# Expert stage: the Silu outputs turned by a transposing DMA from ACT's queue instead of by PE

## The reference, cut to what matters

```
gate_scores = sigmoid(x @ gate_w.T + balance_bias)
topk_scores, topk_idx = top_k(gate_scores, 2)          # 8 experts, 2 for each token
h = silu(einsum('td,ehd->teh', xf, w1))                # 512 -> 1024
expert_out = einsum('teh,edh->ted', h, w2)             # 1024 -> 512
out = x + sum over the two chosen experts of gate * expert_out
```

## Time and profile before

| | us |
|---|---|
| median of three runs | 609.57 |
| lowest and highest | 607.44 and 611.71 |
| the profiled execution | 608.84 |
| its span | 607.0 |
| PE busy, whole span | 516.3 (85%) |
| DVE, ACT, POOL busy | 402.2, 286.3, 116.2 |

### The profile page before, as it was taken

How to read it: one execution, slowest core, us unless ns; L and a number is a source line. 1 busy time by engine, 2 the same in 40 slices (tenths; PEclk the granted TensorE clock), 3 DMA queues, 4 the chain that set the end, 5 groups by cost and what they waited for, 6 DMA issues and landing times.

```text
span 607.0 us, 11363 instructions
## 1 busy us (share of the span) xinstructions
PE 516.3 (85%) x3769; PEld 305.8 (50%) x3770; DVE 402.2 (66%) x897; ACT 286.3 (47%) x449; POOL 116.2 (19%) x89
## 2 busy tenths in 40 slices
PE   5789999999989898954640699999999999999993
PEld 2664657465565675734430344545555445545441
DVE  3789778937979787875976567666563737683330
ACT  0652868685276484747410354453444525552120
POOL 1212113103150301101272002111211121121112
PEclk9899999999999899986855789999999999999997
DMA  8991505000009991062167247876482674623212
GB/s 324 391 382 52 209 8 202 2 1 2 1 23 383 381 381 36 30 208 105 53 246 272 81 152 229 228 220 191 103 238 74 187 192 118 230 52 52 35 35 35
DMA packets 32785, 93.23 MB, mean 154 GB/s; under 512 B 2896, under 2 KB 4080, under 8 KB 28656
## 3 DMA queue, kind: packets, MB, share of 16 engines
q1 hardware_dynamic: 23984, 74.81, 34.3%
q0 software_dynamic: 4304, 9.77, 8.5%
q10 hardware_dynamic: 4464, 8.22, 4.5%
HBM read 63.36 MB, written 29.43 MB: 153 GB/s over the span
## 4 chain that ended last, share of the span: by engine, by line
PE 68%; issue 10%; DVE 8%; ACT 7%; POOL 3%; DMA 2%; SPq 0%; ACTq 0%; POOLq 0%; DVEq 0%
PE bank L685 19%; PE bank L703 18%; PE bank L342 9%; PE bank L510 4%; PE bank L494 2%; PE bank L424 2%; PE bank L544 2%; PE bank L360 2%; PE bank L454 2%; PE bank L404 2%; PE bank L603 2%; PE bank L534 2%; PE bank L475 1%; ACT ctxT_region L733 1%; POOL routed_rows L1587 1%
## 5 line engine op out<-in xcount | busy, mean ns | idle before, releaser
L685 PE MATMUL bank<-wbuf,ctx_region 128*128 x504 | 117.2, 391 | 6.5 <-issue 5.4
L1617 POOL DMA_INDIRECT out<-misc,ints x21 | 40.4, 1922 | 234.7 <-ACT misc L952 174.6
L685 PEld LDWEIGHTS bank<-wbuf,ctx_region 128*128 128x128 f16 x504 | 49.3, 100 | 66.6 <-issue 14.8
L1379 DVE SCALAR_TENSOR_TENSOR wbuf<-ctx_region,wbuf 128x2048 f32 (+1 forms) x28 | 62.9, 2288 | 26.0 <-ACT wbuf L870 26.0
L870 ACT ACTIVATE wbuf<-ctx_region 128x2048 f32 (+1 forms) x28 | 51.9, 1902 | 27.5 <-issue 25.7
L1519 POOL TENSOR_TENSOR small<-small 128x2 f32<-128x2 f32 (+2 forms) x25 | 27.7, 1108 | 191.6 <-DVE small L1010 184.9
L959 ACT ACTIVATE ctxT_region<-bank 128x512 f32<-128x512 f32 x42 | 25.1, 597 | 78.0 <-PE bank L685 78.0
L703 PE MATMUL bank<-wbuf,actT 128*128 x264 | 58.8, 379 | 1.0 <-DVE actT L1480 1.0
L703 PE MATMUL bank<-wbuf,xn 128*128 x240 | 53.4, 379 | 0.0
L510 PE MATMUL bank<-ctx_region,wbuf 128*128 128x256 f16 x384 | 43.3, 273 | 4.3 <-DVE ctx_region L1139 3.4
L1467 DVE COPY ints<-ctx_region 128x1 int32<-128x1 int32 x22 | 3.4, 154 | 60.4 <-PE bank L342 60.4
(11 more groups left out here) (214 smaller groups left out, 879.4 us busy)
## 6 DMA issues: line engine op xcount, KB each, us to landing
ctx_region<-in_experts SPq DMA_DIRECT2D x28, 1024.0 KB, 5.2
routed_rows<-ctxT_region SPq DMA_DIRECT2D x1, 16900.0 KB, 50.6
ctx_region<-in_ctx SPq DMA_DIRECT2D x8, 1536.0 KB, 9.1
ctx_region<-routed_rows ACTq DMA_DIRECT2D x23, 260.0 KB, 2.7
wbuf<-in_experts SPq DMA_DIRECT2D x4, 1024.0 KB, 5.2
out<-x ACTq DMA_DIRECT2D x8, 256.0 KB, 2.6
x<-in_x SPq DMA_DIRECT2D x1, 1536.0 KB, 14.1
wbuf<-in_wqT SPq DMA_DIRECT2D x4, 256.0 KB, 4.4
```

What stands on the lines that cost most here:

```text
L685: mm = nc.tensor.matmul(bank[half][:, :], xgT[:, b, x_part, k * P:(k + 1) * P], w16[:, ds(at + (w_part + k * EH + half * 512), 512)], star ...
L1379: nc.vector.scalar_tensor_tensor(w16[:, ds(at + (LOW + n * PIECE), PIECE)], src_[:, piece], W_SCALE, w16[:, ds(at + (HIGH + n * PIECE), PI ...
L1617: nc.gpsimd.indirect_dma_start(out, bass.IndirectOffsetOnAxis(idx[:, slot_no:slot_no + 1].bitcast(U32), axis=0), y_out[:, slot_no, :], Non ...
```

## The change

The 16 transposes of PE for the hidden tile, and the two copies out of PSUM, are replaced by one DMA that transposes from `h16` to `hT[b]`. ACT issues it behind the two Silus of the tile, after a wait for `h_lo` (DVE's split). S(n) waits for this DMA (`hT`), and so does the split of the next tile, since `h16` is one buffer. The first product alternates between two pairs of banks. On DVE the split of tile n is moved ahead of the copy of the rows of tile n+1.

```diff
-            def hidden_T(tile):
-
-                for part, cut, done in ((0, s["h_hi"], s["hT_ps0"]), (1, s["h_lo"], s["hT_ps1"])):
-                    pe.wait_ge(cut, tile + 1)
-                    transposes(bank[2 + part][:, :].bitcast(F16), [h16[:, part, k * P:(k + 1) * P] for k in range(HC)], done, ident16)
...
-                            mm = nc.tensor.matmul(bank[half][:, :], xgT[:, b, x_part, k * P:(k + 1) * P],
+                            mm = nc.tensor.matmul(bank[2 * b + half][:, :], xgT[:, b, x_part, k * P:(k + 1) * P],
...
-                pe.wait_ge(s["hT0"], tile + 1)
-                pe.wait_ge(s["hT1"], tile + 1)
+                pe.wait_ge(s["hT"], tile * 16 + 16)
...
                         second_product(i * 2 + (u - 1), (u - 1) % 2, experts[u - 1])
-                        hidden_T(i * 2 + u)
...
+            def hidden_T(tile, b):
+
+                act.wait_ge(s["h_lo"], tile + 1)
+                act.sem_inc(s["turning"], 1)
+                act.dma_start(hT[b].rearrange("p a (c t) -> p (a c) t", t=P), h16.rearrange("p a h -> p (a h)"),
+                              transpose=True).then_inc(s["hT"], 16)
...
-            def hidden_copy(tile, b):
-                act.wait_ge(s["hT_ps0"], tile + 1)
-                nc.scalar.copy(hT[b][:, 0, :], bank[2][:, :].bitcast(F16)).then_inc(s["hT0"], 1)
...
                     for u in (1, 2):
                         hidden(i * 2 + u, u % 2)
+                        hidden_T(i * 2 + u, u % 2)
                         cut_next_high(i * 2 + (u - 1), (2, 3))
                         cut_next_high(i * 2 + u, (0, 1))
-                        hidden_copy(i * 2 + u, u % 2)
                         gated(i * 2 + (u - 1), (u - 1) % 2)
...
-            def cut_hidden(tile):
+            def cut_hidden(tile, again=True):
 
                 dve.wait_ge(s["h"], tile * 2 + 2)
+                if again:
+                    dve.wait_ge(s["hT"], tile * 16)
...
-            def hidden_copy(tile, b):
-                dve.wait_ge(s["hT_ps1"], tile + 1)
-                nc.vector.tensor_copy(hT[b][:, 1, :], bank[3][:, :].bitcast(F16)).then_inc(s["hT1"], 1)
...
                     for u in (1, 2):
+                        cut_hidden(i * 2 + u)
                         rows_copy(i * 2 + (u + 1), (u + 1) % 2)
-                        cut_hidden(i * 2 + u)
                         cut_next_low(i * 2 + (u - 1), (2, 3))
                         cut_next_low(i * 2 + u, (0, 1))
-                        hidden_copy(i * 2 + u, u % 2)
                         gate_of(i * 2 + u, u % 2)
```

More of the change, by code:

```diff
@@ L79 @@
 route rt_sel rt_cnt_ps rt_exp rt_slots rt_map zrow_fill zrow xs_zero rows_set scattered
-xg_in0 xg_in1 fields xgT_ps xgT h_ps h h_hi h_lo hT_ps0 hT_ps1 hT0 hT1 y2_ps y2 gate_parts gate idx scat added out_spare
+xg_in0 xg_in1 fields xgT_ps xgT h_ps h h_hi h_lo hT turning y2_ps y2 gate_parts gate idx scat added out_spare
 ident16 finished staged w_hi w1_lo w2_lo""".split()
@@ L710, in _ @@
             rows_T(1, 16)
-            hidden_T(0)
             last = last_of(pe)
@@ L958, in hidden @@
                     act.wait_ge(s["h_ps"], tile * 2 + (half + 1))
-                    nc.scalar.activation(h[:, half * 512:half * 512 + 512], bank[half][:, :], ACT.Silu,
+                    nc.scalar.activation(h[:, half * 512:half * 512 + 512], bank[2 * b + half][:, :], ACT.Silu,
                                          scale=1.0 / W_SCALE).then_inc(s["h"], 1)
-            def hidden_copy(tile, b):
-                act.wait_ge(s["hT_ps0"], tile + 1)
-                nc.scalar.copy(hT[b][:, 0, :], bank[2][:, :].bitcast(F16)).then_inc(s["hT0"], 1)
             gate_exp(1)
@@ L974, in _ @@
             hidden(0, 0)
-            hidden_copy(0, 0)
+            hidden_T(0, 0)
             act.wait_ge(s["w2_lo"], 2)
@@ L1498, in _ @@
             rows_copy(1, 1, again=False)
-            cut_hidden(0)
-            hidden_copy(0, 0)
+            cut_hidden(0, again=False)
             cut_low(stage, 0, (0, 1), W_PIECES)
```

## The result

The changed kernel takes 681.26 us (677.43 to 683.40, four runs) against 608.69 for the kernel before: a ratio of 1.118, 95% interval 1.111 to 1.125. The direction was forecast, the size was not: 638 was predicted, and a loss of 29 us became one of 73. The profiled execution took 677.43 us with a span of 675.6.

What follows compares the result with a forecast made beforehand. PE was taken as the bound. With an issue of 2.9 us, 608.84 + 47.5 (idle PE in cut steps) - 16.9 - 3.4 + 1.0 = 637.0, or 638 against the median; forecast 622 to 655, full range 592 to 693.

Steps and rivals of the forecast that it cites:

- What bounds the kernel: Expert stage: PE, busy 229.3 of 233 us, 12.0 us a tile; ACT and DVE form a chain busy shares don't show.
- What the change removes: PE: 16.9 us of hidden-tile transposes, 3.4 at the head; step 11.1 us; tail -1.3 at Y = 0.34.
- The fixed part of the turn: Cut step on ACT and DVE: split, hand-over, register loads, cuts and low parts take 12.5 us, plus Y.
- F waiting for the rows' copy behind the split: First product on PE waits for DVE's copy: 2 us in a group's first cut step, over 4 in those behind.
- the term Y: Issue time of the transposing DMA on ACT's queue: put at 2.9 us, between a plain 0.34 and 3.84.
- rival C: Issue or landing much dearer: Y = 5.9 gives 693, paying per piece near 890; chance 0.25.
- steps without cuts: Loop steps on ACT: turn in 7.2 + Y, 10.1 us, hidden under PE's 11.1; lengthen from Y = 3.9.
- the cover of 2.1 us a group: Slack before PE needs the rows' copy, once in each of four groups of cut steps: 8.4 us off the loss.
- The landing: Second product's wait for the DMA: lands 2.7 us after issue, may take 8.9; hidden in the loop, tail plus 1.0.
- No idle ahead of S: Sign in the profile after: PE does not stand idle before the second product waiting for the DMA.
- rival D: On top of any: idle gaps of 4 us lower PE's clock, its step becomes 16.6, 16 us more, 654; no separate chance.
- The estimate of some 800: Whole kernel, if 16 blocks of 1309 ns run in a row, 21 us a DMA: 20 steps of 23 us.

Runs made afterwards that it cites:

- e3: Kernel before, with SP loading only a sixteenth of each weight piece of experts 2 to 7: 609.21 us, ratio 1.000.
- e4: Kernel before, PE still transposing, with ACT's wait for the split ahead of the cuts and DVE's split ahead of the rows' copy: 617.62 us, ratio 1.016.
- e7: Changed kernel with the transposing DMA behind the cuts and a sixteenth of the weight loads of experts 2 to 7: 585.79 us, ratio 0.963.
- e2: Changed kernel with SP loading only a sixteenth of each weight piece of experts 2 to 7: 639.0 us, ratio 1.050.
- e9: Changed kernel whose DMA transposes only the high part, 256 KB in place of 512: 623.11 us, ratio 1.024.
- e12: Changed kernel with the transposing DMA as two of 256 KB, high and low part, issued one behind the other: 689.91 us, ratio 1.130.
- e1: Changed kernel with ACT's wait for the split and its transposing DMA moved behind the step's two cuts: 595.87 us, ratio 0.978.
- e5: Changed kernel with a plain 512 KB DMA in place of the transposing one, same place and waits: 614.71 us, ratio 1.011.
- e6: Changed kernel with SP issuing the transposing DMA ahead of a step's weight loads, ACT waiting for the split only before the next Silu: 625.75 us, ratio 1.022.

## Why the prediction was right or wrong

What bounds the kernel, and that ACT's and DVE's idle time is no cover: right. With a sixteenth of the loads the kernel before took the same 609 us (e3), and the wait alone cost it 9 (e4).

What the change removes: right, slightly low. An undisturbed step is 10.8 us instead of the 11.1 used. e7 gained 23 us, where -16.9 - 3.4 - 1.3 = -21.6 was worked out.

The fixed part of the turn, 12.5 us: right in the mean. Measured 12.45, and 12.4 to 13.0 in five more kernels. That it fits to 0.1 is in part luck, since single steps had 11.5 to 13.5.

F waiting for the rows' copy behind the split: right, 52.8 us in 15 waits of up to 5.3, where 47.5 us of idle PE were forecast.

**The step that failed is the term Y.** I took the middle of two indirect DMAs, 2.9 us; the issues of the cut steps measured 4.89 in the mean, from 1.37 to 8.43. The result lies in rival C, a much dearer issue, which had a chance of 0.25. The prediction had a row for it, an issue of SP at the head of the kernel of 4.89 us, and priced it at 672. That the mean is 4.89 too is chance. I read 0.53, the mean busy share of the DMA engines, as half of the time and as a reason not to exclude a stretch. I should have asked what runs in the steps that matter: weights load in most of the steps in which ACT cuts. Nor is the price mainly one of addressing, as I argued. 256 KB take 1.28 us in all steps, and 512 KB 1.4 to 2.1 with the DMA behind the cuts and small loads (e7); the rest comes with what moves beside it (e2, e9, e12).

Two smaller terms hang on it. The three steps without cuts between the cut steps were to be hidden; with issues of 6.3 to 7.6 us they turned in 14.4, 13.0 and 13.1. And since those steps were no shorter than PE's own, the cover of 2.1 us a group, 8.4 in all, was not won back. With these put in, the sum closes: 637.0 + 13 x 2.0 + 7 + 8.4 = 678, where the profiled execution took 677.4. It was made after the fact, and leaves out that PE's step is 10.8 and not 11.1.

The landing: wrong in its price, right in its rank. I took Y + 2.7 = 5.6 us; it was 4.3 alone and 8.6 and 7.2 in the median, at the edge of the 8.9 that the loop allows. "No idle ahead of S" did not come true, and PE waiting there was one of my signs of being wrong: S waited 19.2 us, 12 times, hidden in part behind the longer turns. It decides only in the kernels in which the issue no longer does (e1, e5, e6).

The clock, rival D: it came, at 0.90. 14 of the first and second products took 6.9 to 8.3 us instead of 5.35, all behind a gap of 2.0 us or more; others behind gaps of up to 3.2 us kept 5.35. But PE has room in these turns, so I think it was paid mostly in idle time; the exception is F of tile 18 (7.67 us), which is on the chain. No run tells its price apart.

By the Trainium skill's table in "DMA: Bandwidth & Descriptors" I had estimated 2.7 us of sequencer time for 128 tiles. They are not seen: the whole issue can be over in 1.37. The Trainium skill, "Advanced Engine Details and Errata", X-Bar Transpose, has such DMAs as fast as regular ones: this case agrees roughly for the landing (8.6 and 7.2 against 7.2 and 5.6 us of the plain copy in e5) and not for the issue (1.4 to 8.4 against 0.49). The 1309 ns of the Trainium skill, "VectorE: DVE Perf Modes", The three transpose paths, for one block don't add up over 16 blocks: all of them can land in 4.3 us. (The estimate of some 800 that the prediction made from them is low by its own numbers: 20 steps of 23 us against 11.1 give some 827.)

## What to carry to other kernels

A DMA that replaces compute is paid on the queue that issues it, and what stands behind it there pays; ask how long the issue lasts while other transfers run, and put the work that others wait for ahead of it. Here moving one call behind the cuts turned a loss of 12% into a gain of 2.2%. A chain that closes over two engines (split, issue, cut, low part, split) must be added up as one turn and held against the bound engine's step; busy shares of 43% (ACT) and 58% (DVE) don't show that it is longer.

## What the hardware showed that I had not expected

- The issue of a transposing DMA from SBUF to SBUF took 1.27 to 1.35 us for 256 KB in all 21 steps of e9, beside loads or not. For 512 KB it took 1.4 to 8.4 us as one DMA, and 2.7 to 8.3 as two.
- Loads with rows of 8 KB beside it make it long, in 11 of 12 steps of the changed kernel; the same bytes in rows of 1 KB, and loaded more slowly, brought the mean from 4.89 to 2.87 us.
- The changed kernel's ACT queue moved 48,144 packets against 4,464, some 2,080 for each transposing DMA of 512 KB: pieces of about 256 bytes.
- A plain 512 KB copy from SBUF to SBUF beside the loads lands after 5.6 and 7.2 us in the median by destination (e5).
